# A scan kernel's plan of side steps: room by duration, the softplus laid among the gated unit, and y begun in two parts

## The chip, the cores and the metric

The kernel runs on one core of a Trainium2 chip. The time is the device time of one execution in microseconds; the number compared is the median of several runs. Smaller is better. A core has engines that run their own queues of instructions and wait for each other by semaphores: PE (matrix multiply), DVE (VectorE), ACT (ScalarE), POOL (GpSimd) and SP, which here only starts DMAs.

## The reference

The input is 8 sequences of 256 tokens by 256 channels, all in float32. Each goes through a conditioned transformer layer (attention with 16 heads, then a feed-forward layer with GELU) and then through a conditioned state-space layer, cut to its core here:

```
h, gate = adaln(x, c)                       # layer norm, scaled and shifted by the condition
# once forward, and once on the flipped sequence (backward):
xs, z = split(h @ in_w);  xs = silu(xs)     # 512 channels each
proj  = xs @ xproj_w                        # dt (512), B (64), C (64) per token
dt    = softplus(proj_dt + dt_bias)
for each token t:                           # state: 512 channels x 64 states
    hst = hst * exp(dt_t * A) + (dt_t * x_t) * B_t
    y_t = sum over states of hst * C_t
y = (y + xs * D) * silu(z) @ out_w
x = x + gate * (h_fwd + h_bwd)
h, gate = adaln(x, c)
x = x + gate * ((silu(h @ w1) * (h @ w2)) @ w3)     # the gated unit, glu
```

## The kernel before

The work is written out by hand as one queue for each engine. A block is one sequence of 256 tokens; there are 8 blocks, and each has two **passes** over the 64 states, the forward one (d = 0) and the backward one (d = 1), so 16 passes and 1024 states. Blocks 1 to 6 are the body of a hardware loop; block 0 and block 7 stand outside it.

**The work of a state** n runs over 512 channels x 256 tokens and is cut into two halves (e = 0, 1) of two channel groups each:

- ACT makes the decays `dA = exp(dt*A)` (L567, four instructions a state) two states ahead, and most of the forcing `uBT = u*B` (L553) three states ahead; POOL makes one of four forcing tiles (L417).
- PE transposes the forcing of the next state into PSUM (`force`, L1226), and adds the finished state n-2 into y in PSUM (`sum_state`, L1242).
- DVE scans over the tokens (L893), one instruction for each half. It writes into one of four buffers `hst`.
- POOL multiplies the state by C (`times_C`, L408), one instruction a state, when both scans of the state are done. `sum_state` waits for it.

**The side steps.** All the other work (layer norms, attention, products, softplus, residuals) is cut into numbered steps of named stages: `norm`, `qkv`, `heads`, `proj`, `up`, `down`, `ins` (the input product), `dts` (C, B, dt, softplus and u), `post` (the output product), `glu`. Every engine has a generator for each stage that does its own part of each step. `interleave` issues the two halves of each state and behind half i the steps that the plan gives to it. `order(d, has_prev, has_next)` writes the list of steps of a pass, and `Plan` lays them over the 128 halves: a step of `heads` takes one half, any other step moves the position on by its ROOM times a scale, so that the list ends at half 120. The same plan is used by all engines, so a step stands behind the same half on each of them. In a forward pass the steps are those of the same block's backward input (`own`), of the block before (`last`: output, norm, gated unit) and of the next block (`first`); a backward pass has the output product of its forward pass, and the rest of the next block up to its softplus.

**Softplus** is in steps 15 to 20 of `dts`: ACT does exp at 15 (L509), 1+ at 16 (L512) and ln at 17 (L515); DVE does `expo` at 17 (L815, waits for ACT's 16), `pre` at 18 (L818), `dt` at 19 (L822) and `u = dt*xs` at 20 (L826). These four DVE instructions are 1024 wide and read both operands from SBUF. At 21 PE transposes u, at 22 DVE copies it out (L829).

**y** is begun at half 0 of state 2 of each pass: PE waits until DVE has read the previous y out (`gate_y`, L878, at half 1 of state 2 in DVE's queue) and writes `xs*D` into the two PSUM banks (`start_y`, L1234).

What follows names a half as state.half: 56.1 is the second half of state 56.

Of the kernel before, what the change touches and what calls it, by code (L numbers as in the profile page):

```python
# [18 lines left out]
def cond_transformer_mamba_kernel(  # L19
# [25 lines left out]
    BEHIND = 2  # L45
# [10 lines left out]
    LIGHT, HEAVY, LONG, AMONG = 1.0, 2.0, 2.0, 1.0  # L56
    STEPS = dict(norm=6, qkv=11, heads=37, proj=5, up=12, down=10, ins=12, dts=24, post=10, glu=17)

    ROOM = dict(norm=[HEAVY, LIGHT, HEAVY, HEAVY, LIGHT, LIGHT], qkv=[HEAVY] * 10 + [LIGHT], heads=[LIGHT] * STEPS["heads"],
                proj=[LIGHT, HEAVY, HEAVY, LIGHT, HEAVY], up=[HEAVY] * 8 + [LIGHT, LIGHT, LONG, LIGHT], down=[HEAVY] * 8 + [LIGHT, HEAVY],  # L60
                ins=[HEAVY] * 8 + [LIGHT, LIGHT, LONG, LIGHT], dts=[HEAVY] * 12 + [LIGHT] * 2 + [HEAVY] * 3 + [LONG] + [HEAVY] * 4 + [LIGHT] * 2,
                post=[HEAVY, LIGHT, LIGHT] + [HEAVY] * 4 + [LIGHT, HEAVY, LIGHT], glu=[HEAVY] * 4 + [LIGHT, LONG] + [HEAVY] * 4 + [LIGHT] + [HEAVY] * 4 + [LIGHT, HEAVY])
# [16 lines left out]
    def order(d, has_prev, has_next):  # L79
# [60 lines left out]
    with ctx:  # L140
# [800 lines left out]
        def _(pe):  # L941
# [305 lines left out]
            def state_of(p, d, very_first, very_last):  # L1247
                def state(n, e):
# [5 lines left out]
                    if n == BEHIND and e == 0:  # L1254
                        start_y(p, d)
# [7 lines left out]
            def period(b, has_prev, has_next):  # L1263
# [14 lines left out]
                def free(d, plan):  # L1278
# [3 lines left out]
                    def before(j):  # L1282
# [6 lines left out]
                        if plan.steps[j] == ("own", "dts", 21) and has_prev:  # L1289
                            pe.wait_ge(hT_ready[LN_GLU].sem, hT_ready[LN_GLU].at(b - 1, 1))  # L1290
# [80 lines left out]
```

## Time and profile before

| what | value |
|---|---|
| median of 3 runs | 3443.36 us (3441.26 to 3447.32) |
| the profiled execution | 3439.44 us, its span 3437.6 us |
| busy: PE, DVE, ACT, POOL | 88%, 85%, 87%, 85% of the span |
| POOL's first and last multiplication by C | starts at 201.0 and 3398.3 us |
| forward pass (passes 4 to 12) | 201.0 to 203.1 us |
| backward pass (passes 3 to 13) | 204.0 to 205.1 us |
| first and last forward pass (0, 14) | 188.2 and 190.3 us |

Busy shares say how much of the span an engine had an instruction in work. The time of a pass is the distance between the starts of POOL's multiplications of state 0 in one pass and the next. What lies before the first and after the last has no part in the plan. All windows below are in us from the span's start and begin and end at such a start, so that a window of eight states can be compared with another.

### The profile page before, as it was taken

The page shows a single profiled execution, that of the slowest core. Times are in us where ns is not written, and L with a number is a line of the kernel's source. Part 1 is how long each engine was busy: PE and PEld are TensorE (multiplying, and loading weights), DVE is VectorE, ACT ScalarE, POOL GpSimd, SP SyncE. Part 2 cuts the span into 40 slices and gives each one's busy share as a digit, 9 for nine tenths or more (in the row PEclk, how much of TensorE's full clock was granted, in tenths as well). Part 3 has the DMA queues.
Part 4 walks back from the last instruction along what each step waited for, and adds up shares of the span by engine and source line. Part 5 has one row for each costly group of instructions (what it writes and reads, how often), then busy time and mean ns, then how long its engine had stood idle before and what let it go on. Part 6 is the DMA issues. An engine that isn't in the chain of part 4 may idle for free.

```text
span 3437.6 us, 70222 instructions
## 1 busy us (share of the span) xinstructions
PE 3024.1 (88%) x21944; PEld 2678.1 (78%) x21944; DVE 2913.4 (85%) x3331; ACT 2994.6 (87%) x6469; POOL 2934.5 (85%) x1552
## 2 busy tenths in 40 slices
PE   8788898999988899888998989899998889988776
PEld 6577787888878888787877888788887888877765
DVE  3269988899888998889988998889988899899885
ACT  1189989899889989899999998999988999998994
POOL 0069988899888998889988998889988899899995
PEclk6699999999999999999999999999999999999999
DMA  4011111111111111111111111111111111111211
GB/s 172 0 44 44 47 42 47 41 51 46 42 47 48 46 45 43 47 46 47 44 42 47 49 47 42 49 40 52 46 42 47 48 47 44 43 44 43 54 47 27
DMA packets 163039, 162.55 MB, mean 47 GB/s; under 512 B 17610, under 2 KB 156874, under 8 KB 162644
## 3 DMA queue, kind: packets, MB, share of 16 engines
q1 hardware_dynamic: 162644, 157.69, 16.6%
q8 instruction: 198, 3.24, 0.4%
q14 instruction: 197, 1.61, 0.2%
HBM read 154.44 MB, written 3.18 MB: 46 GB/s over the span
## 4 chain that ended last, share of the span: by engine, by line
PE 29%; POOL 26%; issue 20%; ACT 15%; DVE 7%; DMA 2%; POOLq 0%; DVEq 0%; ACTq 0%; SPq 0%
POOL hst L408 21%; PE ps L1226 7%; ACT dA L567 7%; PE ps L1242 7%; PE ps L994 6%; POOL uBT L417 5%; ACT uBT L553 4%; DVE hst L893 3%; PE ps L1003 2%; DMA C_sb<-c_dram 1%; PE ps L1115 1%; PE ps L1066 1%; DVE qk L826 1%; PE ps L1041 1%; PE ps L1151 1%
## 5 line engine op out<-in xcount | busy, mean ns | idle before, releaser
L408 POOL TENSOR_TENSOR hst<-hst,C_sb 128x1024 f32<-128x1024 f32 x1024 | 2433.4, 2395 | 271.0 <-DVE hst L893 265.6
L893 DVE TENSOR_TENSOR_SCAN hst<-dA,ps 128x512 f32<-128x512 f32 x2048 | 2381.9, 1204 | 165.5 <-PE ps L1226 143.1
L567 ACT ACTIVATE dA<-dt,A 128x255 f32<-128x255 f32 x4096 | 1754.8, 498 | 5.3 <-DVE hst L893 5.2
L1242 PE MATMUL ps<-ident,hst 128*128 128x128 f32 x8192 | 1275.4, 279 | 172.4 <-POOL hst L408 170.8
L1226 PE MATMUL ps<-ident,uBT 128*128 128x128 f32 x8192 | 1280.4, 280 | 107.6 <-DVE hst L893 99.2
L553 ACT ACTIVATE uBT<-uT,BT 128x512 f32<-128x512 f32 x1536 | 1046.8, 715 | 177.8 <-PE ps L1226 168.3
L1226 PEld LDWEIGHTS ps<-ident,uBT 128*128 128x128 f32 x8192 | 996.1, 145 | 255.7 <-DVE hst L893 130.8
L1242 PEld LDWEIGHTS ps<-ident,hst 128*128 128x128 f32 x8192 | 971.0, 143 | 239.9 <-POOL hst L408 237.9
L417 POOL TENSOR_TENSOR uBT<-uT,BT 128x512 f32<-128x512 f32 x512 | 548.9, 1072 | 189.6 <-DVE uT L829 184.9
L476 ACT ACTIVATE probs<-ps,nmax 128x128 f32<-128x128 f32 (+1 forms) x256 | 93.7, 421 | 102.9 <-DVE nmax L764 102.8
L994 PE MATMUL ps<-xsT,w_xp 128*128 128x256 f32 x512 | 130.7, 380 | 2.1 <-ACT qk L505 2.1
L1066 PE MATMUL ps<-qk 32*128 32x256 f32 (+1 forms) x512 | 128.1, 373 | 0.0
L1041 PEld LDWEIGHTS ps<-v,probsT 128*128 128x128 f32 x768 | 105.6, 209 | 9.7 <-issue 7.6
L1041 PE MATMUL ps<-v,probsT 128*128 128x17 f32 x768 | 106.3, 266 | 1.3 <-DVE probsT L758 1.3
L1066 PEld LDWEIGHTS ps<-qk 32*128 32x128 f32 x512 | 82.0, 199 | 19.6 <-issue 2.7
L994 PEld LDWEIGHTS ps<-xsT,w_xp 128*128 128x128 f32 x512 | 87.8, 190 | 9.3 <-ACT qk L505 2.3
L764 DVE TENSOR_REDUCE nmax<-ps 128x2 f32<-128x512 f32 (+1 forms) x128 | 70.8, 553 | 22.0 <-PE ps L1066 19.0
L758 DVE COPY probsT<-ps 128x512 f32<-128x512 f32 (+1 forms) x128 | 68.5, 535 | 18.6 <-PE ps L1050 18.5
L448 ACT ACTIVATE rstd<-mv,eps_col 128x2 f32<-128x2 f32 x32 | 9.4, 295 | 84.1 <-DVE mv L703 84.1
L815 DVE SCALAR_TENSOR_TENSOR qk<-uT,qk 128x1024 f32<-128x1024 f32 x16 | 26.6, 1662 | 60.5 <-ACT uT L512 60.5
L1050 PE MATMUL ps<-ident,probs 128*128 128x128 f32 x384 | 69.1, 292 | 4.5 <-ACT probs L476 4.5
L994 PE MATMUL ps<-hT,w 128*128 128x256 f32 x256 | 70.2, 405 | 1.7 <-DVE hT L711 1.7
(142 smaller groups left out, 2107.0 us busy)
## 6 DMA issues: line engine op xcount, KB each, us to landing
C_sb<-c_dram SPq DMA_DIRECT2D x1024, 128.0 KB, 2.9
gate_l<-gate_rows_dram SPq DMA_DIRECT2D x16, 256.0 KB, 3.7
x_att<-in_x_dram SPq DMA_DIRECT2D x8, 256.0 KB, 3.2
w<-in_L_cond_W_dram SPq DMA_DIRECT2D x2, 1024.0 KB
out_dram<-x_glu SPq DMA_DIRECT2D x8, 256.0 KB, 3.2
wg<-in_L_cond_mlp_w_dram SPq DMA_DIRECT2D x3, 512.0 KB, 11.3
w_xp<-_L_cond_fwd_xproj_w_dram SPq DMA_DIRECT2D x1, 1280.0 KB, 12.2
w_xp<-_L_cond_bwd_xproj_w_dram SPq DMA_DIRECT2D x1, 1280.0 KB, 14.8
```

What stands on the lines that cost most here:

```text
L408: pool.tensor_tensor(h, h, C_sb[:, n % FED:n % FED + 1, :].to_broadcast([P, KI, NB]), ALU.mult).then_inc(hC_ready.sem, 1)
L417: pool.tensor_tensor(uBT[:, n % NF, 1, :], uT[:, d, DI:2 * DI], BT[:, d, 1, n:n + 1].to_broadcast([P, DI]), ALU.mult).then_inc(uBT_pooled. ...
L476: act.activation(probs[:, e, 0:keys], ps[:, BANK_P + g % 2, e * T:e * T + keys], ACT.Exp, bias=nmax[:, e:e + 1]).then_inc(probs_ready.sem, 1)
L553: done = act.activation(uBT[:, n % NF, j, :], uT[:, d, j * DI:(j + 1) * DI], ACT.Copy, scale=BT[:, d, j, n:n + 1])
L567: done = act.activation(dA[:, n % NT, c, lo:hi], dt[:, d, c, lo:hi], ACT.Exp, scale=A[:, d, c, n:n + 1])
L764: dve.tensor_reduce(nmax[:, :], ps[:, BANK_P + g % 2, :].rearrange("p (e t) -> p e t", t=T)[:, :, 0:keys], AX.X, ALU.max, negate=True).the ...
L893: dve.tensor_tensor_scan(pair(hst[:, n % NR]), pair(dA[:, n % NT]), ps[:, BANK_U + (2 * n + e) % (2 * NU), :][:, way], 0.0, ALU.mult, ALU. ...
L994: last = pe.matmul(ps[:, BANK_P + i % 2, 0:NB], lhsT(k), rhs[:, k, :], start=(k == 0), stop=(k == kn - 1))
L1041: last = pe.matmul(ps[:, BANK_P + g % 2, e * (HD + 1):(e + 1) * (HD + 1)], probsT[:, (k * 2 + e) * P:(k * 2 + e + 1) * P], v[:, k, h, :], ...
L1066: last = pe.matmul(ps[:, BANK_P + g % 2, e * T:e * T + keys], qT[rows, c, ti * P:(ti + 1) * P], kT[rows, c, 0:keys], start=False, stop=(e ...
L1226: last = pe.transpose(ps[:, BANK_U + (2 * n + e) % (2 * NU), o:o + P], uBT[:, n % NF, j, c * P:(c + 1) * P], ident[:, :])
L1242: last = pe.matmul(ps[:, BANK_Y + j, c * P:(c + 1) * P], hst[:, n % NR, c, j * P:(j + 1) * P], ident[:, :], start=False, stop=(n == NS - 1 ...
```

## The change

It changes three things. First, the table ROOM has six sizes instead of three: the steps without work get 0.3, one product 1.4 or 0.8, the long instructions of ACT and DVE 2.0 or 4.0. Second, `order` for a forward pass with a predecessor no longer lays the second norm's end among steps 14 to 20 of `dts` and the gated unit behind them: norm steps 4 and 5 stand alone, then the gated unit with `dts` 14 to 20 spread among it, then `dts` 21 to 23. PE's step 21 now waits for the gated unit's residual. Third, `start_y` writes half of the columns at half 0 of state 2 and half of them at half 1.

```
-    LIGHT, HEAVY, LONG, AMONG = 1.0, 2.0, 2.0, 1.0
+    NONE, LIGHT, EVEN, HEAVY, LONG, AMONG = 0.3, 0.8, 1.4, 2.0, 4.0, 1.0
...
-                ins=[HEAVY] * 8 + [LIGHT, LIGHT, LONG, LIGHT], dts=[HEAVY] * 12 + [LIGHT] * 2 + [HEAVY] * 3 + [LONG] + [HEAVY] * 4 + [LIGHT] * 2,
+                ins=[EVEN] * 4 + [LIGHT] * 5 + [NONE, LONG, NONE],
+                dts=[LIGHT] * 4 + [EVEN] * 8 + [LIGHT, NONE, NONE, HEAVY] + [LONG] * 5 + [HEAVY, HEAVY, NONE],
...
-                    + meanwhile(stage("own", "dts", 14, 21), stage("last", "norm", 4, 6))
-                    + stage("own", "dts", 21, STEPS["dts"]) + stage("last", "glu") + first)
+                    + stage("last", "norm", 4, 6) + meanwhile(stage("last", "glu"), stage("own", "dts", 14, 21))
+                    + stage("own", "dts", 21, STEPS["dts"]) + first)
...
-            def start_y(p, d):
-
-                pe.wait_ge(g_ready.sem, g_ready.at(p, 0))
+            def start_y(p, d, e):
+
+                if e == 0:
+                    pe.wait_ge(g_ready.sem, g_ready.at(p, 0))
                 for j in range(TT):
-                    for c in range(KI):
+                    for c in range(2 * e, 2 * e + 2):
...
-                    if n == BEHIND and e == 0:
-                        start_y(p, d)
+                    if n == BEHIND:
+                        start_y(p, d, e)
...
-                            pe.wait_ge(hT_ready[LN_GLU].sem, hT_ready[LN_GLU].at(b - 1, 1))
+                            pe.wait_ge(res_done[RES_GLU].sem, res_done[RES_GLU].at(b - 1, 1))
```

What the plan does to the queues is shown at three places. An instruction of the scan (L893 before, L894 after) is one half of a state; the list of the order names it SCALAR_TENSOR_TENSOR with output `hst`.

DVE's queue in the backward pass of block 0, from the copy of B to the copy of u. Before:

```order
L893 SCALAR_TENSOR_TENSOR hst<-dA,ps 128x512 x12
L815 SCALAR_TENSOR_TENSOR qk<-uT,qk 128x1024
L893 SCALAR_TENSOR_TENSOR hst<-dA,ps 128x512
L818 TENSOR_TENSOR qk<-qk 128x1024
L893 SCALAR_TENSOR_TENSOR hst<-dA,ps 128x512
L822 TENSOR_TENSOR dt<-dt,qk 128x1024
L893 SCALAR_TENSOR_TENSOR hst<-dA,ps 128x512
L826 TENSOR_TENSOR qk<-dt,xsT 128x1024
L893 SCALAR_TENSOR_TENSOR hst<-dA,ps 128x512 x2
L829 COPY uT<-ps 128x1024
```

And of the change:

```order
L894 SCALAR_TENSOR_TENSOR hst<-dA,ps 128x512 x11
L816 SCALAR_TENSOR_TENSOR qk<-uT,qk 128x1024
L894 SCALAR_TENSOR_TENSOR hst<-dA,ps 128x512 x2
L819 TENSOR_TENSOR qk<-qk 128x1024
L894 SCALAR_TENSOR_TENSOR hst<-dA,ps 128x512 x3
L823 TENSOR_TENSOR dt<-dt,qk 128x1024
L894 SCALAR_TENSOR_TENSOR hst<-dA,ps 128x512 x2
L827 TENSOR_TENSOR qk<-dt,xsT 128x1024
L894 SCALAR_TENSOR_TENSOR hst<-dA,ps 128x512 x4
L830 COPY uT<-ps 128x1024
```

The four long instructions stood one half apart, at 56.1 to 58.0; now they stand at 53.1, 54.1, 56.0 and 57.0.

DVE's queue in the forward pass of the loop body; the rows with ISA and REGISTER_ALU are waits and their arithmetic. Before, around the same softplus:

```order
L893 SCALAR_TENSOR_TENSOR hst<-dA,ps 128x512
L815 SCALAR_TENSOR_TENSOR qk<-uT,qk 128x1024
L889 REGISTER_ALU
L890 ISA
L893 SCALAR_TENSOR_TENSOR hst<-dA,ps 128x512
L817 ISA
L818 TENSOR_TENSOR qk<-qk 128x1024
```

And of the change (`gT<-ps,gT` is a product of the gated unit):

```order
L816 SCALAR_TENSOR_TENSOR qk<-uT,qk 128x1024
L891 REGISTER_ALU
L894 SCALAR_TENSOR_TENSOR hst<-dA,ps 128x512
L854 REGISTER_ALU
L855 TENSOR_TENSOR gT<-ps,gT 128x256
L890 REGISTER_ALU
L891 ISA
L894 SCALAR_TENSOR_TENSOR hst<-dA,ps 128x512
L891 REGISTER_ALU
L894 SCALAR_TENSOR_TENSOR hst<-dA,ps 128x512
L818 ISA
L819 TENSOR_TENSOR qk<-qk 128x1024
```

The four long instructions moved from 21.1 to 23.0 to 26.0, 27.1, 28.1 and 30.0, with the second half of the gated unit between them; the unit itself begins at 20.0 instead of 25.0 and ends at 29.0 instead of 32.1.

PE's queue in the backward pass of block 0, at the products for C (L1125) and B (L1132). Before:

```order
L1125 MATMUL ps<-xsT,w_xp 64x256 x2
L1226 MATMUL ps<-ident,uBT 128x128 x4
L1242 MATMUL ps<-ident,hst 128x128 x4
L1132 MATMUL ps<-w_xp,xsT 128x64 x4
L1226 MATMUL ps<-ident,uBT 128x128 x4
L1242 MATMUL ps<-ident,hst 128x128 x4
L1132 MATMUL ps<-w_xp,xsT 128x64 x4
```

And of the change:

```order
L1126 MATMUL ps<-xsT,w_xp 64x256 x2
L1133 MATMUL ps<-w_xp,xsT 128x64 x4
L1227 MATMUL ps<-ident,uBT 128x128 x4
L1244 MATMUL ps<-ident,hst 128x128 x4
L1133 MATMUL ps<-w_xp,xsT 128x64 x4
L995 MATMUL ps<-xsT,w_xp 128x256 x2
```

Two product steps now stand behind one half in places. The twelve products of `dts` 0 to 11 took the halves 48.0 to 54.0 and now take 47.0 to 51.0; in the forward pass they took 12.0 to 18.1 and now take 11.1 to 16.1. Over the passes of the loop body there were no halves with two products before, and there are five in a forward pass and eight in a backward pass now. In the feed-forward part of the backward pass, norm step 4 moved from 29.1 to 30.0 and the first product of `up` from 30.0, behind norm step 5, to 31.0; the GELU from 35.0 to 34.1 and the first product of `down` from 35.1 to 36.0.

## Rows read from the trace of the kernel before

**Rows 1.** The page, part 1: busy time of each engine.

```profile
PE 3024.1 (88%) x21944; PEld 2678.1 (78%) x21944; DVE 2913.4 (85%) x3331; ACT 2994.6 (87%) x6469; POOL 2934.5 (85%) x1552
```

**Rows 2.** Groups by line: busy us, mean ns, idle before it and its releasers.

```profile
L408 POOL TENSOR_TENSOR hst<-hst,C_sb 128x1024 f32<-128x1024 f32 x1024 | 2433.4, 2395 | 271.0 <-DVE hst L893 265.6
L893 DVE TENSOR_TENSOR_SCAN hst<-dA,ps 128x512 f32<-128x512 f32 x2048 | 2381.9, 1204 | 165.5 <-PE ps L1226 143.1 <-ACT dA L567 16.0 <-PE ps L1242 3.6
```

**Rows 3.** Timeline of POOL in an undisturbed stretch (start, length, instruction, count).

```profile
1542.44 1.06 POOL L417 TENSOR_TENSOR uBT<-uT,BT 128x512 f32<-128x512 f32 x1
...
1548.09 1.06 POOL L417 TENSOR_TENSOR uBT<-uT,BT 128x512 f32<-128x512 f32 x1
```

**Rows 4.** Timeline of PE, forward pass, one product behind each half.

```profile
1417.69 0.60 PE L1226 MATMUL ps<-ident,uBT 128*128 128x128 f32 x4
...
1418.57 1.03 PE L994 MATMUL ps<-hT_ssm,w_in 128*128 128x256 f32 x4
1419.43 0.60 PE L1226 MATMUL ps<-ident,uBT 128*128 128x128 f32 x4
```

**Rows 5.** Windows of whole states: length, busy times with counts, PE's clock, DMA.

```profile
1463.85:1488.77 24.92, 17.18 (x123) 15.54 (x121) 20.24 (x19) 23.17 (x49) 18.95 (x10) 0.85 0.15 33
1488.77:1513.99 25.22, 25.22 (x172) 23.25 (x171) 22.73 (x26) 22.05 (x43) 22.78 (x13) 0.94 0.15 43
1679.78:1707.44 27.66, 23.95 (x161) 20.87 (x160) 23.97 (x31) 22.20 (x51) 22.77 (x14) 0.94 0.15 39
1707.44:1734.30 26.86, 26.20 (x188) 23.47 (x186) 21.92 (x23) 24.37 (x46) 22.88 (x12) 1.00 0.19 44
1758.52:1782.48 23.96, 23.96 (x184) 22.03 (x183) 19.17 (x18) 23.53 (x53) 22.77 (x14) 1.00 0.18 48
1782.48:1812.80 30.32, 18.04 (x123) 16.13 (x122) 25.00 (x21) 28.07 (x62) 23.49 (x13) 0.83 0.20 55
3133.28:3165.38 32.10, 22.09 (x133) 19.55 (x134) 31.48 (x22) 24.38 (x51) 24.76 (x14) 0.79 0.15 33
```

**Rows 6.** Timeline of DVE at the softplus of a backward pass.

```profile
1785.41 1.51 DVE L815 SCALAR_TENSOR_TENSOR qk<-uT,qk 128x1024 f32<-128x1024 f32 x1 [3.13 <-ACT uT L512]
1787.97 1.19 DVE L818 TENSOR_TENSOR qk<-qk 128x1024 f32<-128x1024 f32 x1
1790.22 1.19 DVE L822 TENSOR_TENSOR dt<-dt,qk 128x1024 f32<-128x1024 f32 x1
1792.47 2.25 DVE L826 TENSOR_TENSOR qk<-dt,xsT 128x1024 f32<-128x1024 f32 x1
```

**Rows 7.** Timeline of POOL there.

```profile
1790.38 3.25 POOL L408 TENSOR_TENSOR hst<-hst,C_sb 128x1024 f32<-128x1024 f32 x1 [4.54 <-DVE hst L893]
```

**Rows 8.** Timeline of DVE at the softplus of the last forward pass.

```profile
3133.90 6.17 DVE L815 SCALAR_TENSOR_TENSOR qk<-uT,qk 128x1024 f32<-128x1024 f32 x1 [1.40 <-ACT uT L512]
3143.35 2.56 DVE L818 TENSOR_TENSOR qk<-qk 128x1024 f32<-128x1024 f32 x1
```

**Rows 9.** Timeline of POOL there.

```profile
3136.61 2.38 POOL L408 TENSOR_TENSOR hst<-hst,C_sb 128x1024 f32<-128x1024 f32 x1
3142.46 2.36 POOL L408 TENSOR_TENSOR hst<-hst,C_sb 128x1024 f32<-128x1024 f32 x1 [3.47 <-DVE hst L893]
3147.19 2.36 POOL L408 TENSOR_TENSOR hst<-hst,C_sb 128x1024 f32<-128x1024 f32 x1 [0.38 <-DVE hst L893]
3151.90 2.37 POOL L408 TENSOR_TENSOR hst<-hst,C_sb 128x1024 f32<-128x1024 f32 x1 [2.35 <-DVE hst L893]
```

**Rows 10.** Waits from 1679.78 to 1707.44: us in total, times, longest.

```profile
ACT rstd L448 <- DVE mv L703: 3.5, 1, 3.5
PE ps L988 <- ACT probsT L462: 2.0, 1, 2.0
```

**Rows 11.** Timeline of PE at the start of a forward pass's y.

```profile
1412.76 2.05 PE L1234 MATMUL ps<-skip_diag,xsT 128*128 128x128 f32 x16 [0.98 <-DVE gT L878]
```

**Rows 12.** Waits of the whole span, same columns as rows 10.

```profile
DVE qk L815 <- ACT uT L512: 60.5, 16, 9.8
```

More of the change, by code:

```diff
@@ L51, in cond_transformer_mamba_kernel @@
     GATE_SSM, GATE_GLU = 0, 1
-    LIGHT, HEAVY, LONG, AMONG = 1.0, 2.0, 2.0, 1.0
+    NONE, LIGHT, EVEN, HEAVY, LONG, AMONG = 0.3, 0.8, 1.4, 2.0, 4.0, 1.0
     STEPS = dict(norm=6, qkv=11, heads=37, proj=5, up=12, down=10, ins=12, dts=24, post=10, glu=17)
-    ROOM = dict(norm=[HEAVY, LIGHT, HEAVY, HEAVY, LIGHT, LIGHT], qkv=[HEAVY] * 10 + [LIGHT], heads=[LIGHT] * STEPS["heads"],
-                proj=[LIGHT, HEAVY, HEAVY, LIGHT, HEAVY], up=[HEAVY] * 8 + [LIGHT, LIGHT, LONG, LIGHT], down=[HEAVY] * 8 + [LIGHT, HEAVY],
-                ins=[HEAVY] * 8 + [LIGHT, LIGHT, LONG, LIGHT], dts=[HEAVY] * 12 + [LIGHT] * 2 + [HEAVY] * 3 + [LONG] + [HEAVY] * 4 + [LIGHT] * 2,
-                post=[HEAVY, LIGHT, LIGHT] + [HEAVY] * 4 + [LIGHT, HEAVY, LIGHT], glu=[HEAVY] * 4 + [LIGHT, LONG] + [HEAVY] * 4 + [LIGHT] + [HEAVY] * 4 + [LIGHT, HEAVY])
+    ROOM = dict(norm=[HEAVY, NONE, LIGHT, LONG, EVEN, HEAVY], qkv=[EVEN] * 10 + [NONE], heads=[LIGHT] * STEPS["heads"],
+                proj=[LIGHT, HEAVY, HEAVY, NONE, HEAVY], up=[EVEN] * 8 + [LIGHT, NONE, LONG, NONE], down=[EVEN] * 8 + [NONE, HEAVY],
+                ins=[EVEN] * 4 + [LIGHT] * 5 + [NONE, LONG, NONE],
+                dts=[LIGHT] * 4 + [EVEN] * 8 + [LIGHT, NONE, NONE, HEAVY] + [LONG] * 5 + [HEAVY, HEAVY, NONE],
+                post=[HEAVY, HEAVY, NONE] + [EVEN] * 4 + [NONE, LONG, NONE], glu=[EVEN] * 4 + [NONE, LONG] + [EVEN] * 4 + [NONE] + [EVEN] * 4 + [NONE, HEAVY])
     FIRST_HALF, LAST_HALF = 6, 120
```

## The prediction

> **What bounds the kernel now.** I began with the busy times: four engines within four per cent of each other [rows 1], so no single one sets the time, and a shift of work in time matters more than its amount. The groups by line then say which wait stands for lost time. POOL has the longest instruction of a state and no side steps, and 265.6 us of its idle time end with a DVE scan [rows 2]. So the kernel's time is POOL's busy time plus what the side steps make it wait. In an undisturbed stretch POOL does two states in 1548.09 - 1542.44 = 5.65 us [rows 3], so eight in 22.6 and a pass in 180.8. Against this the table ahead has 201 to 203 us for a forward and 204 to 205 us for a backward pass: 20 and 24 us too much.
>
> The windows of eight states say where [rows 5]. In a backward pass: states 24 to 31 27.66 us (5.1 over 22.6), 32 to 39 26.86 (4.3 over), 48 to 55 23.96 (1.4 over), 56 to 63 30.32 (7.7 over). In a forward pass the window from 1463.85 holds the six states 18 to 23 with the softplus, 24.92 us where the floor is 17.0 (7.9 over), and the next one states 24 to 31 with the gated unit, 25.22 us (2.6 over).
>
> The timelines give two reasons. **PE's pace:** a half with a product takes 1419.43 - 1417.69 = 1.74 us, of which the product is 0.86 and the state's own work 0.88 [rows 4]; POOL's floor for a half is 5.65/4 = 1.41. One product in every half makes PE the bound, and less than 0.6 products a half leave POOL the bound. **The softplus on DVE:** four long instructions one half apart, 1.51 + 1.19 + 1.19 + 2.25 = 6.14 us, behind a wait of 3.13 us for ACT [rows 6]; that wait is 60.5 us in 16 softplus [rows 12]. From L818 to L822 lie 2.25 us for one long instruction and one scan [rows 6], 1.12 us each, so between side steps DVE gains only 0.29 us a half on POOL.
>
> **What the change moves.** No instruction is added or taken away. The sum is made in POOL's lost time, pass by pass, against the profiled execution (3439.44 us; the median shown is 3.9 us higher, and I add that at the end).
>
> *Softplus of a backward pass.* Spread as ordered (53.1, 54.1, 56.0, 57.0), the wait for ACT loses its reason: ACT's 1+ stands two halves ahead of DVE's `expo` instead of one, and gets 1.4 of the 3.1 us back, the rest from ACT's lag being smaller by then; I take all of it as gone, 3.1 us. But the four instructions then meet a busy POOL. When POOL idles they take 1.19 us; when POOL is in the middle of its multiplication, they last until it ends and 1.19 more: 2.25 to 2.56 us [rows 6, 8]. One that starts together with POOL's multiplication stretches that to 3.25 us instead of 2.37 [rows 7]. The last forward pass is a test already made: its long instructions stand three, two and two halves apart (37.1, 39.0, 40.0, 41.0), and its eight states take 32.10 us, 9.5 over the floor [rows 5]: not less than the 7.7 of the dense chain. There `expo` lasted 6.17 us, while POOL did three instructions in a row, and POOL's next multiplication came 3142.46 - 3136.61 = 5.85 us after the one before, 3.0 over the floor; the following ones came 4.73 and 4.71 us apart [rows 8, 9], 1.9 over each. What decides is the half: all three that cost 1.9 stand behind a first half, where POOL is in mid-instruction. Behind a second half POOL starts with them and pays 3.25 - 2.37 = 0.9 [rows 7]. For the new places I therefore count 0.9 for 54.1, 1.9 each for 56.0 and 57.0, and for `expo` at 53.1 between 0.9 and 3.0, say 1.3, since it comes out of a stretch where PE has held POOL back and no backlog waits there. Sum 6.0 instead of 7.7.
>
> The Trainium skill (page "SBUF — State Buffer", section "Who interferes with whom") states what these rows show: a VectorE instruction with two SBUF inputs contends with a GpSimd one that reads SBUF, and whichever is first keeps the other out for its whole length. The trace agrees (3.25 us against 2.37). By this rule alone every one of the four is to meet POOL wherever it stands; an estimate by it leaves the softplus at its 7.7 and the sum at about 3430.
>
> *Products of `dts`, backward pass.* PE's time for the twelve and the state work of their halves: before 13 halves, (13 + 12) x 0.87 = 21.8 against POOL's 18.4; now 9 halves (47.0 to 51.0), (9 + 12) x 0.87 = 18.3 against 12.7. PE falls behind by 5.6 us in place of 3.4, and the 3.4 showed as 1.4 us lost [rows 5]; so 2.0 us are taken by the buffers, and 3.6 are lost now: 2.2 more. The free halves that follow do not give them back, since POOL cannot run faster than its floor. They do cover a part of `expo`'s cost; I count 1.2 more. The `ins` products, 6 halves in place of 8, cost 0.87 x 14 - 1.41 x 6 = 3.7 in place of 2.6: 1.0 more.
>
> *Norm and feed-forward, backward pass.* PE waits 2.0 us for the normalised tokens, and ACT 3.5 us for the statistics [rows 10]. Norm step 4 one half later takes 1.4 of PE's wait away, and norm step 5 no longer stands in front of `up` 0 in the same half; the GELU gets three halves ahead of `down` instead of one. Of the 5.1 + 4.3 us over the floor in states 24 to 39 [rows 5] I count 3.0 as gained, with two halves of doubled products costing 0.5 of it: 2.5.
>
> Backward pass: -1.7 + 1.2 + 1.0 - 2.5 = -2.0 us, seven such passes with a successor: -14.
>
> *Forward pass.* The same four instructions go among the gated unit at 26.0 (first half), 27.1, 28.1 (second), 30.0 (first). There DVE also has the unit's copies, so its own sum is the better bound: in the sixteen halves of states 24 to 31 it has 16 x 1.12 of scans, the long ones at 1.19 to 2.56 (7.5 with waits), the copy of u 1.2, four products of 0.4 and a residual of 1.4: 29.6 against 22.6, 7.0 over. Before, the two stretches together were 7.9 + 2.6 = 10.5 over. Gain 3.5. Against it: `ins` and `dts` denser (five doubled halves, 0.87 each, half of it taken by buffers): 2.0; norm 4 and 5 in one half, so DVE waits for PE's transpose in it: 1.0. Net -0.5, six passes: -3.
>
> *First and last forward passes.* The last: its four stand at 47.0, 49.1, 52.0, 54.0, four or five halves apart, in which DVE wins 1.2 us back: 3.0 + 0.7 + 0.7 + 0.7, say 5.5 with a share of chance, in place of 9.5: -4. The first: all four behind second halves, two states apart: -3.
>
> *`start_y`.* Its 2.05 us stand ahead of the transposes that the scan of 3.1 waits for [rows 11]. Half of it moved behind them lets that scan begin about 1 us earlier. But PE's queue is full from there to state 10 of a forward pass, and its sum is the same: nothing lasts there. A backward pass may keep it, since its next states have fewer products: bounds 0 and 1 us, I take 0.1 a pass: -1.
>
> *Sum:* -14 - 3 - 7 - 1 = -25 us: 3439.4 - 25 = 3414, and with 3.9 on it 3418.
>
> **The rivals.** *A. Spreading removes the chain's cost.* If DVE's instructions found POOL's gaps, only DVE's own time over POOL's would be left: twelve halves, 12 x 1.12 + 4 x 1.19 + 1.2 = 19.4 against 16.9, 2.5 over in place of 7.7, and with the norms some 7 us for every pass: 15 x 7 = 105 less, 3340. For it: the wait of 60.5 us, and PE's clock of 0.83 and 0.85 in the windows of the chain [rows 5], low after PE's waits, which would go away too. Against it: the last forward pass, 9.5 us over when spread. Chance 0.15.
>
> *B. Dense products take more than is gained.* Thirteen doubled halves a block at 0.87, none of it taken by buffers, are 11.3 us; 1.2 + 1.0 + 0.5 + 2.0 = 4.7 are already charged. That is 6.6 more a block, and for six and a half blocks 43: 3418 + 43 = 3461. It decides where PE's lag passes 2 us, as in 47.0 to 51.0 and in 3.0 to 6.0 of the forward pass, where DVE's copies wait for the product behind the same half. For it: these are the stretches in which PE is busy all the time (23.96 of 23.96 us, [rows 5]). Against it: in 48 to 55 two thirds of the lag were absorbed. Chance 0.28.
>
> *C. Both cancel:* it needs only `expo` at 3.0 instead of 1.3 in each of 13 passes, 22 us of my 25: 3440. Chance 0.15.
>
> My forecast has 0.42 (3395 to 3435).
>
> **How the numbers follow.** A difference within 0.2%, 7 us, is about what a measurement of this kernel can't tell from none. Faster: A 0.15, the forecast's 0.40, a part of C: 0.56. Same: 0.15. Slower: B and the forecast's own upper tail: 0.29. The range reaches from between A and the forecast to B: 3365 to 3470, with 0.2 outside.
>
> **What the profile would show.** Right: the wait of L816 for ACT under 20 us in total; the four long instructions at 2.2 us or more where they stand behind a first half, and more of POOL's multiplications at 3.25 us; the backward pass near 203, the forward pass near 201; states 48 to 55 of the backward pass above 25 us; states 24 to 39 near 52. Rival A shows 1.19 us for the four and passes near 197. Rival B shows PE busy without a gap in states 3 to 10 and 43 to 52, DVE waiting for L995 and L1116, and forward passes above 205. The forecast is wrong if the places behind a half do not set the price, or if DVE's lead is larger than I read it.

## The result and the profile after

| | before | after |
|---|---|---|
| median of 4 runs, us | 3443.12 (3441.26 to 3447.32) | 3481.55 (3475.43 to 3484.93) |
| ratio to before, 95% interval | | 1.0113, 1.0101 to 1.0125 |
| backward pass, passes 3 to 13, us | 204.0 to 205.1 | 210.3 to 211.9 |
| forward pass, passes 2 to 12, us | 199.6 to 203.1 | 199.9 to 203.1 |
| first and last forward pass, us | 188.2 and 190.3 | 187.4 and 187.5 |

The change costs 38 us, where 25 were forecast as a gain. It is lost in the backward passes: seven with a successor, at 5.6 us each (means 205.0 and 210.6), are 39 us. The forward passes lose 0.5 each (201.7 and 202.2), 3 us, and the first and the last give 3.6 back. One execution each of `e3_y` (6029 us), `e5_late` (4008 us) and `e9_front` (7478 us) was in a slow state and is left out of the medians below; the 3455 us and the 26 us that expectations give for `e5_late` still count it.

Part 1 of the page of after answers to [rows 1]: the same instructions, with nearly the same busy times.

```profile
PE 3030.0 (87%) x21944; PEld 2647.1 (76%) x21944; DVE 2932.0 (84%) x3331; ACT 2995.8 (86%) x6469; POOL 2941.6 (85%) x1552
```

Its groups by line answer to [rows 2] (busy, mean ns, idle before and its releasers). POOL's waits for a scan went from 265.6 to 305.3 us, 39.7 more: about the whole loss. The reading that the time is POOL's work plus what the side steps make it wait holds.

```profile
L409 POOL TENSOR_TENSOR hst<-hst,C_sb 128x1024 f32<-128x1024 f32 x1024 | 2436.8, 2399 | 306.1 <-DVE hst L894 305.3
L894 DVE TENSOR_TENSOR_SCAN hst<-dA,ps 128x512 f32<-128x512 f32 x2048 | 2373.2, 1203 | 145.0 <-PE ps L1227 110.6
```

The waits of after that moved (us in total, times, longest), by the side of [rows 12]:

```profile
DVE sz L805 <- PE ps L1116: 38.5, 32, 1.9
DVE xsT L801 <- PE ps L995: 34.0, 21, 3.0
DVE qk L816 <- ACT uT L513: 30.4, 14, 9.8
...
DVE qk L787 <- PE ps L995: 24.0, 22, 2.2
```

The wait for ACT's 1+ fell from 60.5 to 30.4 us. In its place DVE waits for side products: the three such rows were 20.6, 15.2 and 10.2 us before, 46.0 in all, and are 96.5 now. Its wait for the last product of the residuals (L722 on L1004) went from 44.8 to 63.8 us besides.

The windows of after say where. They are cut like those of [rows 5], in the backward pass of the fourth block (length; PE, PEld, DVE, ACT, POOL; PE's clock; DMA): states 24 to 31, 32 to 39, 44 to 51, 52 to 59.

```profile
1697.54:1723.62 26.08, 22.92 (x164) 19.51 (x163) 23.33 (x31) 20.72 (x48) 22.71 (x13) 1.00 0.14 41
1723.62:1753.52 29.90, 28.18 (x190) 23.83 (x188) 22.70 (x28) 24.32 (x51) 22.79 (x12) 1.00 0.15 36
1765.65:1794.06 28.41, 28.25 (x191) 23.36 (x190) 20.81 (x22) 25.59 (x51) 22.84 (x13) 1.00 0.14 41
1794.06:1824.68 30.62, 21.48 (x148) 17.88 (x145) 29.36 (x22) 28.04 (x60) 24.62 (x12) 0.89 0.12 35
```

Those of before with the same states as the last two:

```profile
1746.12:1769.82 23.70, 23.70 (x168) 19.56 (x166) 20.69 (x22) 22.53 (x44) 22.68 (x12) 1.00 0.21 49
1769.82:1801.61 31.79, 24.88 (x174) 23.03 (x172) 25.74 (x22) 29.33 (x63) 23.77 (x14) 0.84 0.12 34
```

States 24 to 31 gained 1.6 us in this pass (1.2 in the mean) and the softplus 1.2. States 32 to 39 lost 3.0 and the states with the twelve `dts` products 4.7. Means over the loop's passes, in us, for before, after and the kernels of the next section (backward passes 5 to 13, with four windows of states, and forward passes 4 to 12; the floor is 22.6 us for eight states, 33.9 for twelve):

| kernel | 24 to 31 | 32 to 43 | 44 to 51 | 52 to 59 | backward pass | forward pass |
|---|---|---|---|---|---|---|
| before | 27.6 | 38.7 | 23.7 | 31.8 | 205.0 | 201.7 |
| after | 26.4 | 42.0 | 28.4 | 30.6 | 210.6 | 202.2 |
| e1_table | 26.4 | 42.0 | 28.4 | 30.6 | 210.6 | 203.6 |
| e2_order | 28.3 | 38.7 | 23.7 | 31.8 | 205.7 | 200.5 |
| e3_y | 27.3 | 38.7 | 23.7 | 31.8 | 204.6 | 202.8 |
| e5_late | 24.9 | 40.2 | 28.6 | 30.6 | 207.5 | 201.4 |
| e6_odd | 26.1 | 42.0 | 28.4 | 29.0 | 208.6 | 201.8 |
| e7_both | 24.9 | 40.2 | 28.6 | 29.0 | 205.9 | 200.3 |
| e9_front | 26.7 | 41.2 | 23.7 | 31.8 | 206.5 | 203.0 |
| e15_lean | 24.9 | 40.2 | 26.2 | 30.6 | 205.1 | 201.2 |
| e12_port | 26.7 | 42.0 | 28.4 | 25.0 | 205.3 | 202.3 |
| e14_before_port | 27.6 | 38.7 | 23.7 | 30.4 | 203.6 | 201.3 |
| e10_best | 25.6 | 40.0 | 23.7 | 31.8 | 204.2 | 200.5 |
| e13_psum | 25.2 | 40.0 | 23.7 | 30.9 | 203.0 | 200.4 |

From state 32 to 59 the loop's passes of one kernel repeat within 0.1 us. States 24 to 31 are longer by 1.6 us or more in some passes of a kernel (26.1 and 27.7 in after), and its forward passes differ by 2 us and more, so a difference of 1 us between two forward means says little by itself.

Timelines of after show the two kinds of new stalls. The first is DVE at the end of `up`, whose steps 7 and 8 stand behind one half (34.0). In DVE's queue step m copies product m - 1 (L787), so two copies stand there ahead of the next scan, and the second is of the product that PE makes behind the same half. It waits 1.25 us for it, and the scan after it with it; `up` 2 and 3 behind 32.0 cost the same 1.25 us:

```profile
1728.02 0.48 DVE L787 TENSOR_SCALAR qk<-ps,col_in 128x256 f32<-128x256 f32 x1
1729.76 0.48 DVE L787 TENSOR_SCALAR qk<-ps,col_in 128x256 f32<-128x256 f32 x1 [1.25 <-PE ps L995]
1730.16 1.21 DVE L894 TENSOR_TENSOR_SCAN hst<-dA,ps 128x512 f32<-128x512 f32 x1
```

The residual of `down` (L722) waits longest. It stands behind 39.0, one half behind the last product instead of two:

```profile
1747.56 0.70 DVE L722 TENSOR_TENSOR ps<-ps,gate_l 128x512 f32<-128x512 f32 x1 [2.69 <-PE ps L1004]
```

The second stall is PE in the `dts` products, where two stand behind one half (L1126 for C, L1133 for B):

```profile
1776.17 1.08 PE L1126 MATMUL ps<-xsT,w_xp 128*64 128x256 f32 x4
1777.17 1.10 PE L1133 MATMUL ps<-w_xp,xsT 128*128 128x64 f32 x8
1778.12 0.60 PE L1227 MATMUL ps<-ident,uBT 128*128 128x128 f32 x4
1778.56 0.60 PE L1244 MATMUL ps<-ident,hst 128*128 128x128 f32 x4
```

That half takes PE from 1776.17 to 1778.99, where the next product begins: 2.8 us against POOL's 1.41. PE is busy for 28.25 of 28.41 us in this window, 4.6 us more than before, and the window is 4.7 us longer.

### The profile page after: what moved, and what is told of

It is laid out like the page before. It is cut to its first block, busy times and chain, and to the rows that moved or that the text cites. A ratio compares the mean times of both kernels' runs of the same rounds, so it can differ in the third digit from the quotient of the medians.

```text
span 3478.6 us, 70211 instructions
## 1 busy us (share of the span) xinstructions
PE 3030.0 (87%) x21944; PEld 2647.1 (76%) x21944; DVE 2932.0 (84%) x3331; ACT 2995.8 (86%) x6469; POOL 2941.6 (85%) x1552
## 4 chain that ended last, share of the span: by engine, by line
POOL 41%; issue 29%; PE 18%; ACT 7%; DVE 3%; DMA 2%; POOLq 1%; DVEq 0%; SPq 0%; ACTq 0%
POOL hst L409 32%; POOL uBT L418 9%; PE ps L995 4%; PE ps L1244 4%; PE ps L1227 4%; ACT dA L568 4%; ACT uBT L554 2%; DVE hst L894 2%; DMA C_sb<-c_dram 1%; PE ps L1067 1%; PE ps L1004 1%; PE ps L1042 1%; PE ps L1051 1%; PE ps L1126 1%; PE ps L1133 1%
## 5 line engine op out<-in xcount | busy, mean ns | idle before, releaser
L409 POOL TENSOR_TENSOR hst<-hst,C_sb 128x1024 f32<-128x1024 f32 x1024 | 2436.8, 2399 | 306.1 <-DVE hst L894 305.3
L894 DVE TENSOR_TENSOR_SCAN hst<-dA,ps 128x512 f32<-128x512 f32 x2048 | 2373.2, 1203 | 145.0 <-PE ps L1227 110.6
L1244 PEld LDWEIGHTS ps<-ident,hst 128*128 128x128 f32 x8192 | 954.1, 142 | 346.0 <-POOL hst L409 344.7
L1227 PEld LDWEIGHTS ps<-ident,uBT 128*128 128x128 f32 x8192 | 979.1, 144 | 238.8 <-DVE hst L894 118.5
L995 PE MATMUL ps<-xsT,w_xp 128*128 128x256 f32 x512 | 129.9, 381 | 0.1
L995 PEld LDWEIGHTS ps<-xsT,w_xp 128*128 128x128 f32 x512 | 88.4, 190 | 7.7 <-ACT qk L506 0.4
L722 DVE TENSOR_TENSOR ps<-ps,gate_l 128x512 f32<-128x512 f32 x40 | 27.6, 690 | 63.8 <-PE ps L1004 63.8
L995 PE MATMUL ps<-hT,wg 128*128 128x256 f32 x256 | 67.4, 391 | 1.5 <-DVE hT L712 1.2
```

Of the source, the lines that this page charges most:

```text
L409: pool.tensor_tensor(h, h, C_sb[:, n % FED:n % FED + 1, :].to_broadcast([P, KI, NB]), ALU.mult).then_inc(hC_ready.sem, 1)
L894: dve.tensor_tensor_scan(pair(hst[:, n % NR]), pair(dA[:, n % NT]), ps[:, BANK_U + (2 * n + e) % (2 * NU), :][:, way], 0.0, ALU.mult, ALU. ...
L995: last = pe.matmul(ps[:, BANK_P + i % 2, 0:NB], lhsT(k), rhs[:, k, :], start=(k == 0), stop=(k == kn - 1))
L1227: last = pe.transpose(ps[:, BANK_U + (2 * n + e) % (2 * NU), o:o + P], uBT[:, n % NF, j, c * P:(c + 1) * P], ident[:, :])
L1244: last = pe.matmul(ps[:, BANK_Y + j, c * P:(c + 1) * P], hst[:, n % NR, c, j * P:(j + 1) * P], ident[:, :], start=False, stop=(n == NS - 1 ...
```

## The experiments

The parts of the change come first, each alone, then each suspected cost. What lies before the first state differs by up to 5.6 us between the profiled executions (196.1 us in `e3_y`, 201.0 in before, 201.7 in `e1_table`), so the passes decide here and not the spans, and a difference of less than 5 us between two medians can come from there. The kernel before was run again beside each group of experiments and had medians of 3442.74, 3441.75 and 3442.05 us.

**e1_table** is before with the new table ROOM and nothing else.

> The kernel before with the new table ROOM alone; order and start_y as before. Two theories of why the change is 38 us slower. Theory D (dependence): time is lost where DVE has to take a product that PE makes behind the same half, since PE is behind DVE and DVE's next scan then stands behind the copy; 1 to 2 us for each such half. Theory P (density): time is lost because PE has more products in a stretch than POOL's pace allows, 0.87 us for each surplus product, whoever takes it. Both put the loss into the table: backward passes as in the changed kernel, 210 us in place of 205, and seven of them give +37. With the old order the forward passes have more halves with two products (glu and qkv among them), 9 in place of 5: D expects forward passes of 206 to 210, the whole 3500 to 3530. P expects forward passes of 203 to 205, the whole 3485 to 3500.

Measured: 3489.04 us, 1.0139 (1.0120 to 1.0158). Its backward passes are those of the change, window by window, so the whole loss comes from the table; in the forward pass the table costs 1.9 us. The whole and the forward pass of 203.6 us are what theory P expected; D's 206 to 210 us did not come.

**e2_order** is before with the new order of a forward pass and the wait that goes with it.

```
-                    + meanwhile(stage("own", "dts", 14, 21), stage("last", "norm", 4, 6))
-                    + stage("own", "dts", 21, STEPS["dts"]) + stage("last", "glu") + first)
+                    + stage("last", "norm", 4, 6) + meanwhile(stage("last", "glu"), stage("own", "dts", 14, 21))
+                    + stage("own", "dts", 21, STEPS["dts"]) + first)
```

> The kernel before with the new order of the forward pass alone (and PE's wait of step 21 on the residual that goes with it). Backward passes stay at 205. In forward passes the gated unit's end and the softplus are now mixed, one product to a half at most. By the price of the long instructions (1.9 us behind a first half, 0.9 behind a second) the dense chain's 8 us over the floor become 5 to 8: forward passes 198 to 201, the whole 3420 to 3443. The rival, that the chain costs what it costs wherever it stands: forward passes 201 to 204, the whole 3440 to 3455.

Measured: 3433.58 us, 0.9967 (0.9953 to 0.9981). The forward pass is 1.2 us shorter, and `e10_best` and `e13_psum`, which have this order with the same old places, agree (200.5 and 200.4 us). With the table the gain is gone: the two together stand at 202.2. In the profiled execution the six forward passes with a predecessor win 8.6 us, and the backward passes lose 5.8, in states 24 to 31; whether the order causes that loss was not followed, so the 9 us of the medians are not the order's price alone.

**e3_y** is before with `start_y` in two parts.

> The kernel before with start_y in two parts alone. Sum of the prediction: 0 in forward passes, since PE's queue is full up to state 10, and 0 to 1 us in a backward pass: 3436 to 3443. The rival: the second half of start_y delays the first side step's product behind 3.0, on which the queue of PE stands anyway, and nothing moves: 3443.

Measured: 3441.22 us, 1.0000 (0.9990 to 1.0009). Nothing.

**e5_late** is after, but in DVE's queue alone a step that takes a product made behind the same half goes one half later. PE's queue stays as it is, with its doubled halves.

```
+            at_pe = {i: list(steps) for i, steps in enumerate(self.behind)}
+            for i in range(2 * NS - 1):
+                here = self.behind[i]
+                for k, j in enumerate(here):
+                    chain, name, m = self.steps[j]
+                    source = (chain, name, TAKEN.get((name, m)))
+                    if late and (source in [self.steps[l] for l in at_pe[i]] or (name, m) in ODD and i % 2 == 0):
+                        self.behind[i], self.behind[i + 1] = here[:k], here[k:] + self.behind[i + 1]
+                        break
```

`TAKEN` names the step whose product a step takes: the one before it, in `qkv`, `up`, `ins`, `glu`, `dts` 2, 4, 22, `norm` 5 and `down` 9 (there step 8 has no product; the edit puts the residual two halves behind the last one). `ODD` is empty here. `late` is set for DVE.

> The changed kernel with the same queues on PE, ACT and POOL; only in DVE's queue a step that takes a product of PE's from the same half stands one half later (ins, up, qkv, down 9, dts 2 and 4, norm 5: eight places in a backward pass, five in a forward pass). PE's density is untouched. Theory D: the stalls of DVE in these halves go, 0.7 to 1.5 us each, backward passes 203 to 206 in place of 210.3, forward passes 199 to 201; the whole 3415 to 3450. Theory P: PE's queue is the same and so is the time, 3470 to 3485.

Measured: 3453.49 us, 1.0040 (1.0026 to 1.0054), between the two theories: 28 us of the 38 are back, of which the seven backward passes hold 7 x 3.1 = 22. Waits in states 32 to 39 of after:

```profile
POOL hst L409 <- DVE hst L894: 7.0, 3, 3.8
...
DVE ps L722 <- PE ps L1004: 2.7, 1, 2.7
```

and of e5_late:

```profile
POOL hst L422 <- DVE hst L907: 1.8, 3, 1.1
...
DVE ps L735 <- PE ps L1017: 0.9, 1, 0.9
```

Windows of e5_late, states 44 to 51 and 52 to 59:

```profile
1745.84:1774.45 28.61, 28.61 (x196) 23.97 (x195) 21.23 (x22) 26.08 (x52) 22.86 (x13) 1.00 0.16 41
1774.45:1805.05 30.60, 20.52 (x148) 16.57 (x145) 29.34 (x22) 28.03 (x60) 24.60 (x12) 0.94 0.13 35
```

In states 24 to 43 the stall is DVE's dependence on a product made just ahead: 3.3 us of a backward pass go with it, and these states then take 65.1 us, 1.2 less than before. In states 44 to 51 it is not: PE is busy for 28.61 of 28.61 us, and nothing is gained.

**e6_odd** is after, with a long softplus instruction of DVE that stood behind a first half moved one half later (`ODD` holds `dts` 17 to 20, `TAKEN` is empty): 56.0 to 56.1, 57.0 to 57.1, and 26.0 and 30.0 in the forward pass.

> The changed kernel; only in DVE's queue the long instructions of the softplus that stood behind a first half stand one half later, behind the second, where POOL's multiplication starts with them: 56.0 to 56.1 and 57.0 to 57.1 in a backward pass, 26.0 to 26.1 and 30.0 to 30.1 in a forward pass. If the place in the state sets the price as the prediction has it (1.9 us behind a first half, 0.9 behind a second), each of the four gives 1.0 us: backward passes 208.3 in place of 210.3, the whole 3481 - 26 = 3455. If it does not, or if the whole collision is paid by whoever is late anyway: 3475 to 3485.

Measured: 3458.41 us, 1.0053 (1.0036 to 1.0070), 23 us under the change. The place within the state has a price: states 52 to 59 fall from 30.6 to 29.0. The passes hold 7 x 2.0 + 6 x 0.5 = 17 of the 23 us. Of the rest, 4.4 us lie before the first state, which the profiled execution reaches at 196.8 us where that of after needs 201.2; this edit moves nothing there, so they are chance.

**e7_both** joins the last two.

> The changed kernel with both edits in DVE's queue at once: takings one half later, and the long softplus instructions behind second halves. Alone they gave 26 and 23 us. If the two losses are in different places of a pass and independent, they add: 3481 - 26 - 23 = 3432. If one feeds on the other's slack: 3440 to 3455.

Measured: 3431.60 us, 0.9975 (0.9964 to 0.9985). The savings add up: 28 + 23 = 51, and 50 are measured; in a backward pass 3.1 + 2.0 = 5.1, and 4.8 are measured. The two causes are apart.

**e9_front** is after, but in a backward pass the steps from `ins` 0 (43.0) to the end stand where before had them.

```
+                if d == 1 and has_next:
+                    i = old[j] if j >= self.steps.index(('first', 'ins', 0)) else new[j]
```

> The changed kernel, but from ins step 0 on (43.0) the backward passes have the places of before: single products, and the four long softplus instructions one half apart at 56.1 to 58.0. This tells the back part of the change (dense products, spread softplus) from its front part (norm, up, down). In the traces states 44 to 59 took 55.4 us before and 59.0 in the change: if the parts are independent, backward passes lose 3.6 us of their 210.3, 206.7, and the whole is 3481 - 25 = 3456. If the spread softplus was worth what rival A said (5 us), the passes stay at 210 or get worse.

Measured: 3451.89 us, 1.0027 (1.0017 to 1.0037). States 44 to 51 are back at 23.7, the softplus at 31.8. So the new places from `ins` on cost 4.1 us a pass net, although the softplus by itself is better off.

**e15_lean** asks whether PE's work is what counts there. It is e5_late, with each step of the `dt` product made in backward passes (d = 0) multiplying one of its two input groups, so half of that sum is left out; places and dependences stay.

```
-                        last = product(m, lambda k: w_xp[d][:, k, m * P:(m + 1) * P], xsT, range(i % 2 * 2, i % 2 * 2 + 2), KI)
+                        last = product(m, lambda k: w_xp[d][:, k, m * P:(m + 1) * P], xsT, range(i % 2 * 2, i % 2 * 2 + 2) if d else (i % 2 * 3,), KI)
```

> The kernel with DVE's takings one half later (3455 us), where each of the eight dt product steps of a backward pass multiplies one of its two channel groups only, which leaves half of the sum out: 0.43 us of PE's time less a step, 3.5 us a pass, with all places and waits as they were. There states 44 to 51 took 28.6 us with PE busy in all of them, against 23.7 before. If PE's surplus is what is lost in these states, they take 25.1 to 25.8 us and the whole is 3455 - 7 x 3 = 3434. If DVE's waits or ACT's load (14.2 us busy of 14.9 in states 48 to 51) hold them, they stay at 28 us and above and the whole at 3450 to 3455.

Measured: 3432.22 us, 0.9973 (0.9963 to 0.9983), 21 us under e5_late, of which 7 x 2.4 = 17 in states 44 to 51 of the backward passes. Its window of states 44 to 51:

```profile
1738.08:1764.29 26.21, 25.42 (x180) 20.84 (x179) 20.97 (x22) 24.34 (x50) 22.83 (x13) 1.00 0.16 44
```

PE has 28.61 - 25.42 = 3.2 us less to do and the eight states are 2.4 us shorter. There PE's pace is the cause: three quarters of what is taken from PE comes back, and 2.5 us over the 23.7 of before remain.

**e12_port** and **e14_before_port** measure the softplus's meeting with POOL. In after and in before, the second operand of DVE's four long instructions of a backward pass is read from two banks of PSUM instead of SBUF (and the sum of step 19 is a maximum). These kernels leave out the correction of the softplus and the right factor of u, so their output is another.

```
+                other = lambda t: t if d else ps[:, BANK_P:BANK_P + 2, :].rearrange("p a (k n) -> p (a k) n", n=NB)
...
-                        dve.tensor_tensor(pre, pre, expo, ALU.subtract).then_inc(soft_step.sem, 1)
+                        dve.tensor_tensor(pre, pre, other(expo), ALU.subtract).then_inc(soft_step.sem, 1)
```

> The changed kernel, where in the softplus of the next block's forward input (done in backward passes) the second operand of the four long DVE instructions is read from PSUM, where unrelated values stand, and the sum in dt is a maximum; this leaves the softplus correction and u out, so the output is another, and the sizes, places and waits are the same. It takes away only that both operands come from SBUF. If the price of the spread instructions is a collision with POOL's reads of SBUF, all four take 1.2 us and states 52 to 59 of a backward pass take 25 to 27 us in place of 30.6: passes 205 to 207, the whole 3445 to 3460. If they cost what DVE's own time costs, nothing moves: 3475 to 3485.

> The kernel before with the dense softplus, where in the softplus made in backward passes the second operand of the four long DVE instructions is read from PSUM (unrelated values; the softplus correction and u are left out, the sum in dt is a maximum). It prices the collision with POOL in the dense chain: in the trace of before the four take 6.14 us in place of 4 x 1.2, and one of POOL's multiplications 3.25 in place of 2.37. If those are the whole price, states 52 to 59 of a backward pass take 29.5 us in place of 31.8 and the whole is 3443 - 7 x 2.2 = 3427. If the wait for ACT (3.1 us) sets the chain alone: 3438 to 3443.

Measured: e12_port 3442.55 us, 1.0006 (0.9996 to 1.0015), 39 us under the change and a little under what was expected; e14_before_port 3425.39, 0.9949 (0.9933 to 0.9966), 17 under before. The groups by form of e12_port, with the forward passes' two SBUF operands first (busy, mean ns, idle before):

```profile
L828 DVE TENSOR_TENSOR qk<-dt,xsT 128x1024 f32<-128x1024 f32 x8 | 21.6, 2699 | 0.0
...
L820 DVE TENSOR_TENSOR qk<-qk 128x1024 f32<-128x1024 f32 x8 | 15.3, 1918 | 0.0
...
L820 DVE TENSOR_TENSOR qk<-qk,ps 128x1024 f32<-128x1024 f32 x8 | 9.6, 1199 | 0.0
L828 DVE TENSOR_TENSOR qk<-dt,ps 128x1024 f32<-128x1024 f32 x8 | 9.6, 1199 | 0.0
```

With one operand in PSUM the eight of each group take 1.20 us (1.22 for `expo`) wherever POOL is. Its window of states 52 to 59:

```profile
1772.22:1797.19 24.97, 18.78 (x148) 15.59 (x145) 23.71 (x22) 24.97 (x54) 22.76 (x13) 1.00 0.15 43
```

The spread softplus costs 2.4 us over the floor without the meeting, and 8.0 with it: 5.6 us, in seven passes 39. In before's chain the edit takes only 1.4 off the 31.8, where 2.2 were expected; the other 7.8 over the floor are not this meeting.

**e10_best** puts together what gained: the new order, start_y in two parts and late takings; before's places in the loop's forward passes and, in a backward pass, from `ins` 0 on; the new table elsewhere.

> What the first runs point to, put together: the new order with the old table in forward passes of the loop (and the new table in the first and last forward pass), in backward passes the new table up to norm step 5 at 42.1 and the old one from ins step 0 on, start_y in two parts, and DVE's takings one half later where they shared a half with their product. By windows: forward passes 200.5; backward passes 205.0 with 1.2 us less in states 24 to 43, 203.8; first and last forward pass 187.4. The whole 3442.7 - 6 x 1.2 - 7 x 1.2 - 3.7 = 3423. If the parts disturb each other: 3435 to 3450.

Measured: 3422.30 us, 0.9955 (0.9940 to 0.9970), as expected.

**e13_psum** is e10_best with the whole computation, in which the correction that DVE makes at step 18 of a backward pass is written to PSUM and read from there at step 19.

```
+            def soft(d):
+
+                return pre if d else ps[:, BANK_P:BANK_P + 2, :].rearrange("p a (k n) -> p (a k) n", n=NB)
...
-                        dve.tensor_tensor(pre, pre, expo, ALU.subtract).then_inc(soft_step.sem, 1)
+                        dve.tensor_tensor(soft(d), pre, expo, ALU.subtract).then_inc(soft_step.sem, 1)
...
-                        dve.tensor_tensor(dt[:, d], dt[:, d], pre, ALU.add).then_inc(dt_ready.sem, 1)
+                        dve.tensor_tensor(dt[:, d], dt[:, d], soft(d), ALU.add).then_inc(dt_ready.sem, 1)
```

> The best version so far (3422 us) with one thing more: in the softplus made in backward passes DVE writes the correction (step 18) to PSUM and adds it from there (step 19), so that step 19 no longer reads both operands from SBUF. POOL's multiplication that starts with it was 3.25 us long. If that collision goes, states 52 to 59 take 0.9 us less in each of seven passes: 3416. If the time only moves to step 20, whose u = dt * xs still reads both from SBUF: 3420 to 3424.

Measured: 3411.14 us, 0.9906 (0.9890 to 0.9923), the fastest of all. States 52 to 59 fall by 0.9 us, as expected, which is 6 us in seven passes; of the 11 us under e10_best the other 5 have no cause shown. The sum of step 19 in its two forms, forward and backward:

```profile
L858 DVE TENSOR_TENSOR dt<-dt,qk 128x1024 f32<-128x1024 f32 x8 | 20.2, 2529 | 0.0
...
L858 DVE TENSOR_TENSOR dt<-dt,ps 128x1024 f32<-128x1024 f32 x8 | 9.6, 1194 | 0.0
```

## Why the prediction was wrong

**What bounds the kernel** was read rightly: POOL's waits for scans grew by what the kernel lost, and PE's pace and the softplus on DVE are two of the three places that the experiments move. The third, DVE's waits for products, I did not price.

**Norm and feed-forward, "2.5" gained: the step that failed.** States 24 to 39 were forecast near 52 and take 26.08 + 29.90 = 55.98, against 54.52 before [rows 5]. The gain itself was there: with the stalls gone in e5_late, states 24 to 31 take 24.9 us, 2.7 less than before, where I had counted 3.0 for both windows. What I priced wrongly is "two halves of doubled products costing 0.5". There are three (`up` 2 and 3 at 32.0, `down` 0 and 1 at 36.0, `down` 6 and 7 at 38.1), and at 0.87 us of PE's time each they are 2.6 us, so 0.5 took most of it as absorbed without a reason. Above all, DVE had no part in the price. A step of DVE that takes a product stands ahead of the next scan, and when its product is made behind the same half or one half earlier, the scan waits with it: 1.25 us twice at `up`, 2.7 us at `down`. e5_late shows the cost: 3.3 us a pass in states 24 to 43 with PE's queue untouched, 2.8 of them in states 24 to 39. Those 16 states then take 53.5 us, 0.95 less than before and 1.55 short of the 2.5 that I forecast. This rest stands in states 32 to 39, which are still 1.8 us longer than before, with PE busy for 28.05 of 28.63 us; that PE's pace is its cause there too was not tested.

**Products of `dts` and `ins`, "2.2 more" and "1.0 more": right in kind, too small.** States 44 to 51 lost 4.7 and 40 to 51 together 5.0, where 3.2 was the sum of the two terms. Of the 2.2 I charged only 1.2, since the rest was to cover a part of `expo`; no run shows such a cover. I let the buffers take 2.0 us of PE's lag, since that is what they took before. e15_lean shows that PE's work is what counts: three quarters of what is taken from it comes back. Why less was absorbed than before stays open. What should have warned me is that the stretch had PE busy for 23.96 of 23.96 us already [rows 5].

**Softplus, backward, 7.7 to "6.0": -1.7, measured -1.2** (states 52 to 59 stood 9.2 us over the floor and stand 8.0 over it now). The mechanism was right. Four rows of before (busy, mean ns, idle before):

```profile
L826 DVE TENSOR_TENSOR qk<-dt,xsT 128x1024 f32<-128x1024 f32 x16 | 34.3, 2141 | 0.0
...
L815 DVE SCALAR_TENSOR_TENSOR qk<-uT,qk 128x1024 f32<-128x1024 f32 x16 | 26.6, 1662 | 60.5 <-ACT uT L512 60.5
...
L818 DVE TENSOR_TENSOR qk<-qk 128x1024 f32<-128x1024 f32 x16 | 21.9, 1368 | 0.0
L822 DVE TENSOR_TENSOR dt<-dt,qk 128x1024 f32<-128x1024 f32 x16 | 20.5, 1282 | 0.0
```

and of after:

```profile
L827 DVE TENSOR_TENSOR qk<-dt,xsT 128x1024 f32<-128x1024 f32 x16 | 39.0, 2441 | 0.0
L816 DVE SCALAR_TENSOR_TENSOR qk<-uT,qk 128x1024 f32<-128x1024 f32 x16 | 38.9, 2433 | 30.4 <-ACT uT L513 30.4
L823 DVE TENSOR_TENSOR dt<-dt,qk 128x1024 f32<-128x1024 f32 x16 | 35.3, 2207 | 0.0
...
L819 DVE TENSOR_TENSOR qk<-qk 128x1024 f32<-128x1024 f32 x16 | 25.0, 1562 | 0.0
```

The means add up to 6.45 us before and 8.64 after: sixteen softplus keep DVE busy for 35 us more, while it waits for ACT 30 us less. The timeline of a backward pass of after has the single ones:

```profile
1797.47 3.38 DVE L816 SCALAR_TENSOR_TENSOR qk<-uT,qk 128x1024 f32<-128x1024 f32 x1 [1.26 <-ACT uT L513]
...
1803.01 1.19 DVE L819 TENSOR_TENSOR qk<-qk 128x1024 f32<-128x1024 f32 x1
...
1807.48 3.35 DVE L823 TENSOR_TENSOR dt<-dt,qk 128x1024 f32<-128x1024 f32 x1
...
1812.99 2.49 DVE L827 TENSOR_TENSOR qk<-dt,xsT 128x1024 f32<-128x1024 f32 x1
```

and POOL's at the first two:

```profile
1797.40 2.36 POOL L409 TENSOR_TENSOR hst<-hst,C_sb 128x1024 f32<-128x1024 f32 x1
1803.16 3.27 POOL L409 TENSOR_TENSOR hst<-hst,C_sb 128x1024 f32<-128x1024 f32 x1 [3.40 <-DVE hst L894]
```

From one of POOL's starts to the next lie 5.76 us, 2.9 over the floor of 2.82: `expo` costs 2.9, not the 1.3 I took, since POOL starts 0.07 us ahead of it and keeps it out; DVE's wait for ACT, which I took as gone, is still 1.26 us here. The others come to 1.4, 1.8 and 1.8 (I had 0.9, 1.9, 1.9), in all 8.0 over the floor where 6.0 were counted. The price by place within the state held (e6_odd gained 2.0 us a backward pass, its expectation), and so did the rule of the Trainium skill beside it (page "SBUF — State Buffer", section "Who interferes with whom"). The same section states that a VectorE instruction with at most one SBUF input does not contend outside the two-port modes; e12_port and e13_psum agree, at 1.20 and 1.19 us.

**Forward pass, "-0.5" each, measured +0.5.** The difference is within the spread of the forward means. Two parts, both larger, cancel: the order gains 1.2 (e2_order), the denser table takes 1.9 (e1_table against before). **First and last, "-3" and "-4":** -0.8 and -2.8. **`start_y`, "-1":** nothing, inside its bounds.

**The rivals.** B has the right cause and still too small a price: 3461 against 3481. It counted PE's time for each doubled half and named DVE's copies only for the forward pass; DVE stops for them in the backward pass's feed-forward too. Of its signs, PE with hardly a gap in 44 to 51 and DVE waiting for L995 and L1116 came; forward passes above 205 did not. A is refuted by the rows above: three of the four are longer than 1.19 us, and no pass came near 197. Of the forecast's own signs, the long instructions of 2.2 us and more, the larger number of multiplications over 3 us on POOL (20 against 15) and states 48 to 55 above 25 us (30.5) came; the wait for ACT under 20 us, the backward pass near 203 and states 24 to 39 near 52 did not. The range ended at 3470, since no case priced the two ways of a doubled half together.

## What to carry to other kernels

A plan that lets steps share a slot has to be priced on every queue that takes part. The engine that makes the products is priced by its sum of work in the stretch. The engine that takes them is priced by order: a step that waits for its product holds up the critical instruction that stands behind it in the queue. Where a slot must be doubled, shift the taking queue by one slot; here that alone was worth 28 us. And before a table of sizes is changed as a whole, run it apart from what comes with it: here the new order shortened each forward pass by 1.2 us, which the table hid.

## What was not expected of the hardware

Whether DVE's long instruction or POOL's multiplication is stretched is decided by 0.1 us of start: with POOL 0.07 us ahead, DVE's took 3.38 us and POOL's 2.36; with DVE 0.15 us ahead, DVE's took 1.19 and POOL's 3.27. With one of an instruction's two operands in PSUM it did not happen: 1.20 us in e12_port, and 1.19 us for step 19 in e13_psum. PE's mean granted clock rose from 0.950 to 0.964 while the kernel got slower: 1.00 against 0.94 in states 24 to 31 of the pass shown, 1.00 in both kernels in states 44 to 51, and 0.89 against 0.84 in states 52 to 59. Why it rose was not tested. The clock was no sign of the time here.
